# A similarity whose left side is not normalised, and a load moved behind the norms' row in SyncE's queue

## The reference, cut to what matters

```python
# x: after the attention block, plus its residual; _gn is a group norm
xf  = _gn(x).reshape(B, C, N).transpose(0, 2, 1)
xn  = xf / max(norm(xf, axis=-1), 1e-12)
sim = einsum('bnc,bmc->bnm', xn, xn)          # 1024 x 1024 per sample
val, idx = top_k(sim, 9)
v   = val / (val.sum(-1) + 1e-6)
# twice: xt = feat @ w; out[n] = sum_k v[n,k] * xt[idx[n,k]] + b
#        group norm with 4 groups, then silu
x   = x + out
```

## Time and profile before

| | before |
|---|---|
| median of 3 runs | 685.54 us (684.87 to 685.59) |
| the profiled execution | 687.54 us |
| its span, first to last instruction | 685.7 us |
| TensorE busy | 621.9 us (91%) |
| VectorE busy | 536.6 us (78%) |
| GpSimd busy | 499.2 us (73%) |
| ScalarE busy | 449.2 us (66%) |
| mean granted TensorE clock | 0.98 |

### The profile page before, as it was taken

One profiled execution on the slowest core, in us unless ns is written; L12 is line 12 of the kernel. 1 busy time (PEld: TensorE's weight loads), 2 busy tenths in 40 slices (PEclk: granted clock), 3 DMA queues, 4 the chain that ended last, 5 costly groups with the idle time before them and its releaser, 6 DMA issues.

```text
span 685.7 us, 12336 instructions
## 1 busy us (share of the span) xinstructions
PE 621.9 (91%) x3824; PEld 310.4 (45%) x3824; DVE 536.6 (78%) x1008; ACT 449.2 (66%) x942; POOL 499.2 (73%) x534
## 2 busy tenths in 40 slices
PE   8878899898999999898999999999999999899874
PEld 6654535353444535353544435353535444333441
DVE  3357879788898889797888988898898988857821
ACT  2356477685868767784868768786868686743321
POOL 0224877788797978879797978788897979786810
PEclk9999999999999999999999999999999999979997
DMA  3002533434353535444363634445353534353411
GB/s 94 1 17 46 115 72 79 88 83 96 81 110 69 109 77 110 80 90 92 80 109 62 113 79 108 87 87 100 91 94 63 109 77 98 74 108 78 63 32 31
DMA packets 148722, 55.76 MB, mean 81 GB/s; under 512 B 138008, under 2 KB 138512, under 8 KB 148656
## 3 DMA queue, kind: packets, MB, share of 16 engines
q1 hardware_dynamic: 148656, 54.97, 39.6%
HBM read 12.87 MB, written 4.32 MB: 25 GB/s over the span
## 4 chain that ended last, share of the span: by engine, by line
PE 33%; POOL 24%; issue 16%; DVE 10%; DMA 9%; ACT 7%; SPq 1%; POOLq 0%; ACTq 0%; DVEq 0%
PE pC L974 18%; POOL adj L389 10%; PE pS L930 5%; POOL adj L384 5%; DMA rbc<-rn_row 4%; DMA rn_row<-rnT 4%; ACT adj L527 2%; PE pB L775 2%; DVE kstat L607 2%; ACT ek L458 2%; POOL res L407 2%; PE pA L814 2%; POOL qn L348 2%; POOL xn L372 2%; DVE top L683 2%
## 5 line engine op out<-in xcount | busy, mean ns | idle before, releaser
L974 PE MATMUL pC<-adj,xt 128*64 128x512 f32 x992 | 233.1, 603 | 2.9 <-POOL adj L395 1.6
L389 POOL TENSOR_TENSOR adj<-maskT,adj 128x128 f32<-128x128 f16 (+3 forms) x127 | 163.5, 1287 | 27.0 <-DMA maskT<-mask 25.2
L683 DVE MAX8 top<-pS 128x8 f32<-128x1024 f32 x128 | 155.6, 1224 | 33.1 <-ACT adj L527 32.9
L701 DVE MATCH_REPLACE8 mask<-top,pS 128x1024 uint16<-128x1024 f32 x128 | 155.2, 1213 | 0.0
L930 PE MATMUL pS<-xn 64*128 64x512 f32 x256 | 146.9, 661 | 7.3 <-issue 6.5
L930 PE MATMUL pS<-xn,xsw 64*128 64x512 f32 x256 | 146.2, 662 | 2.9 <-DVE mask L701 2.9
L527 ACT COPY adj<-pS 128x1024 f32<-128x1024 f32 x128 | 128.3, 1003 | 30.3 <-PE pS L932 30.2
L384 POOL TENSOR_TENSOR adj<-maskT,adj 128x128 f32<-128x128 f16 (+6 forms) x111 | 128.4, 1157 | 0.0
L974 PEld LDWEIGHTS pC<-adj,xt 128*64 128x64 f32 x992 | 64.0, 137 | 103.3 <-issue 94.7
L395 POOL TENSOR_TENSOR adj<-adj,selves 128x128 f32<-128x128 f32 x127 | 58.5, 461 | 8.7
L932 PEld LDWEIGHTS pS<-mark,place 64*128 64x128 f16 x256 | 24.7, 97 | 77.3 <-issue 77.3
(11 more groups left out here) (154 smaller groups left out, 1097.0 us busy)
## 6 DMA issues: line engine op xcount, KB each, us to landing
xs<-x SPq DMA_DIRECT2D x32, 128.0 KB, 2.8
vbc<-v_row SPq DMA_DIRECT2D x32, 128.0 KB, 2.9
rbc<-rn_row SPq DMA_DIRECT2D x30, 128.0 KB, 2.9
xsw<-xn SPq DMA_DIRECT2D x30, 128.0 KB, 2.3
out<-res SPq DMA_DIRECT2D x30, 128.0 KB, 2.3
maskT<-mask SPq DMA_TRANSPOSE x128, 3.1
cst<-packed SPq DMA_DIRECT2D x1, 471.5 KB, 3.6
y1sw<-y SPq DMA_DIRECT2D x2, 128.0 KB, 2.3
```

The lines of the kernel that those rows point to most:

```text
L389: pool.tensor_tensor(above, m[:, r, 0:r + 1, :].bitcast(F16), above, ALU.mult).then_inc(done["upper"], 1)
L683: dve.max(top[b % 2][:, r, 0:TOP], pS[r % 2][:, :]).then_inc(done["tile_top"], 1)
L701: dve.match_replace(out=mask[n % MASKS][:, :], in_to_replace=top[b % 2][:, r, 0:TOP], in_values=pS[r % 2][:, :], imm_value=ONE_BITS).then_ ...
L974: mm = pe.matmul(ps[h * C:(h + 1) * C, 0:H], xt[:, t % NJ, t // NJ, :], adj[b % 2][:, t, h * H:(h + 1) * H], start=(t == 0), stop=(t == NT ...
```

## The change

Three things change.

The left side of the similarity is y1 in place of `xn` (and `xsw` is y1 with swapped halves). A block of `pS` then holds the similarity times the norm of the row's token. A positive factor per row leaves the order in the row alone, so the tops and masks are found as before; ScalarE's copy to `adj` takes the inverse norm as its scale, and VectorE multiplies the eight tops of each token by it once per sample. The constants are set anew so that the mark stays large beside the products. y1 and `rn` get two buffers each, y1sw goes, and `rn` waits for what still reads its older buffer.

The swapped copy now waits for y1 and no longer for `xn`. In SyncE's queue it is the first step of `unit`, at 111.8545, where it was the last, at 139.8554.

The load of a later sample moves in SyncE's queue from 0 to 19 behind the sample's begin: before it stood in front of the norms' row of the sample three earlier (122.814), now it stands behind it.

```diff
--- before.py
+++ after.py
@@ -15,9 +15,9 @@
 P = 128
 HEADS = 4
 TOP = 8
-XSCALE = 0.25
+XSCALE = 2.0 ** -12
 SSCALE = XSCALE * XSCALE
-MARK = -2.5 * SSCALE
+MARK = -2.5 / 16
 EPS = 1e-5
 ONE_BITS = 15360.0
 
@@ -34,8 +34,8 @@
           485.0099, 525.4191, 565.7534, 605.859]
 TIMES = {
     "sync": {
-        "attend": [0],
-        "unit": [122.814, 124.0739, 139.8554],
+        "attend": [19],
+        "unit": [111.8545, 122.814, 124.0739],
         "neighbours": [144.5435, 146.5376, 153.5254, 159.4181, 159.4182, 168.0831, 180.5052, 181.0079],
         "convolve": [199.2326, 199.2327, 265.073],
     },
@@ -155,13 +155,12 @@
 
         attn = sb("attn", [P, H])
         x1 = [sb(f"x1_{i}", [P, H]) for i in range(XBUFS)]
-        y1 = sb("y1", [P, H])
+        y1 = [sb(f"y1_{i}", [P, H]) for i in range(2)]
         sq = sb("sq", [P, H])
         xn = [sb(f"xn{i}", [P, H]) for i in range(2)]
-        y1sw = sb("y1sw", [P, H])
         xsw = [sb(f"xsw{i}", [P, H]) for i in range(2)]
         ssq = sb("ssq", [P, NT])
-        rn = sb("rn", [P, NT])
+        rn = [sb(f"rn{i}", [P, NT]) for i in range(2)]
         rnT = sb("rnT", [NT, P])
         rbc = sb("rbc", [P, H])
         st = {n: sb(f"st_{n}", [P, 16]) for n in ("in", "at", "mi", "g1", "g2")}
@@ -205,9 +204,9 @@
             ky_ps ky_copied m_ps m_copied att_ps att_copied
             at_stat at_aggr at_spread at_mean_ps at_minus at_dev at_veps at_rstd at_scale at_bias at_normed x1_ready
             mi_stat mi_aggr mi_spread mi_mean_ps mi_minus mi_dev mi_veps mi_rstd mi_bias y1_ready
-            sq_ready ss_ps ss_read rn_ready rows exchanged first_swapped rn_T rnT_copied rn_saved rn_back xn_ready swapped0 swapped1
+            sq_ready ss_ps ss_read rn_ready rows rn_T rnT_copied rn_saved rn_back xn_ready swapped0 swapped1
             xt1_ps xt1_copied sim_ps sim_copied self_ready tile_top tile_mask turned0 turned1 turned2 diagonal upper lower late_lower late_upper late_diagonal late_y late_res
-            v_tot v_rec v_T vT_copied v_saved v_back
+            top_scaled v_tot v_rec v_T vT_copied v_saved v_back
             g1_ps g1_read g1_stat g1_aggr g1_shift g1_spread g1_mean_ps g1_minus g1_dev g1_veps g1_rstd g1_scale g1_bias
             y2_ready xt2_ps xt2_copied tile_used
             g2_read g2_stat g2_aggr g2_shift g2_spread g2_mean_ps g2_minus g2_dev g2_veps g2_rstd g2_scale g2_bias
@@ -231,10 +230,6 @@
         def row_read(b):
 
             return of("xn_ready", 0) if b == 0 else of("rnT_copied", b - 1)
-
-        def swapped(b):
-
-            return (done["first_swapped"], 1) if b == 0 else of_buffer("swapped", b - 2 if b % 2 == 0 else b, 2, 32)
 
         def weave(engine, *stages):
             live = []
@@ -266,11 +261,12 @@
                                        .unsqueeze(0).broadcast_to([C, H]))
 
             def unit(b):
+                yield
+                sp.wait_ge(*of("y1_ready", b))
+                sp.wait_ge(*of("sim_ps", b - 2, NT))
+                for h in range(2):
+                    sp.dma_start(xsw[b % 2][(1 - h) * C:(2 - h) * C, :], y1[b % 2][h * C:(h + 1) * C, :]).then_inc(done[f"swapped{b % 2}"], 16)
                 if b == 0:
-                    yield
-                    sp.wait_ge(*of("y1_ready", b))
-                    for h in range(2):
-                        sp.dma_start(y1sw[(1 - h) * C:(2 - h) * C, :], y1[h * C:(h + 1) * C, :]).then_inc(done["exchanged"], 16)
                     return
                 yield
                 sp.wait_ge(*of("rnT_copied", b - 1))
@@ -280,11 +276,6 @@
                 sp.wait_ge(*of("xn_ready", b - 1))
                 for dma in spread(rn_row, rbc, b):
                     dma.then_inc(done["rn_back"], 16)
-                yield
-                sp.wait_ge(*of("xn_ready", b))
-                sp.wait_ge(*of("sim_ps", b - 2, NT))
-                for h in range(2):
-                    sp.dma_start(xsw[b % 2][(1 - h) * C:(2 - h) * C, :], xn[b % 2][h * C:(h + 1) * C, :]).then_inc(done[f"swapped{b % 2}"], 16)
 
             def neighbours(b):
                 for r in range(NT):
@@ -359,7 +350,9 @@
                 rstd(b, "mi")
                 yield
                 pool.wait_ge(*of("ss_read", b, 2))
-                pool.tensor_tensor(rn[:, :], ssq[:, :], minus_half[:, :], ALU.pow).then_inc(done["rn_ready"], 1)
+                pool.wait_ge(*of("sim_copied", b - 2, NT))
+                pool.wait_ge(*of("v_tot", b - 2))
+                pool.tensor_tensor(rn[b % 2][:, :], ssq[:, :], minus_half[:, :], ALU.pow).then_inc(done["rn_ready"], 1)
                 yield
                 if b == 0:
                     return
@@ -367,9 +360,7 @@
                 pool.wait_ge(*of("rn_back", b - 1, 32))
                 pool.wait_ge(*of("xt1_ps", b - 2))
                 pool.wait_ge(*of("sim_ps", b - 2, NT))
-                if b > 2:
-                    pool.wait_ge(*swapped(b - 2))
-                pool.tensor_tensor(xn[b % 2][:, :], y1[:, :], rbc[:, :], ALU.mult).then_inc(done["xn_ready"], 1)
+                pool.tensor_tensor(xn[b % 2][:, :], y1[b % 2][:, :], rbc[:, :], ALU.mult).then_inc(done["xn_ready"], 1)
 
             def weights(b):
                 a, m = adj[b % 2], maskT[b % 2]
@@ -499,12 +490,12 @@
                 deviation(b, "mi", pB)
                 yield
                 act.wait_ge(*of("mi_bias", b))
-                act.wait_ge(*of("xn_ready", b - 1))
-                act.activation(y1[:, :], x1[b % XBUFS][:, :], ACT.Identity, bias=st["mi"][:, 15:16],
+                act.wait_ge(*of("sim_ps", b - 2, NT))
+                act.activation(y1[b % 2][:, :], x1[b % XBUFS][:, :], ACT.Identity, bias=st["mi"][:, 15:16],
                                scale=st["mi"][:, 13:14]).then_inc(done["y1_ready"], 1)
                 yield
                 act.wait_ge(*of("y1_ready", b))
-                act.activation(sq[:, :], y1[:, :], ACT.Square).then_inc(done["sq_ready"], 1)
+                act.activation(sq[:, :], y1[b % 2][:, :], ACT.Square).then_inc(done["sq_ready"], 1)
 
             def itself(b):
                 for r in range(NT):
@@ -522,9 +513,10 @@
                     n = NT * b + r
                     yield
                     act.wait_ge(*of_tile("sim_ps", n))
+                    act.wait_ge(*of("rn_ready", b))
                     if b >= 2:
                         act.wait_ge(*of_tile("tile_used", n - 2 * NT))
-                    act.copy(adj[b % 2][:, r, :], pS[r % 2][:, :]).then_inc(done["sim_copied"], 1)
+                    act.activation(adj[b % 2][:, r, :], pS[r % 2][:, :], ACT.Copy, scale=rn[b % 2][:, r:r + 1]).then_inc(done["sim_copied"], 1)
 
             def silu(b, tag, src, dst, signal):
                 yield
@@ -665,10 +657,7 @@
                 yield
                 if b == 0:
                     dve.wait_ge(done["rows"], 1)
-                    dve.tensor_tensor(xn[0][:, :], pB[:, :], y1[:, :], ALU.mult).then_inc(done["xn_ready"], 1)
-                    dve.wait_ge(done["rows"], 2)
-                    dve.wait_ge(done["exchanged"], 32)
-                    dve.tensor_tensor(xsw[0][:, :], pC[:, :], y1sw[:, :], ALU.mult).then_inc(done["first_swapped"], 1)
+                    dve.tensor_tensor(xn[0][:, :], pB[:, :], y1[0][:, :], ALU.mult).then_inc(done["xn_ready"], 1)
                 else:
                     dve.wait_ge(*of("rn_T", b - 1))
                     dve.wait_ge(*of("rn_saved", b - 2, 16))
@@ -683,6 +672,12 @@
                     dve.max(top[b % 2][:, r, 0:TOP], pS[r % 2][:, :]).then_inc(done["tile_top"], 1)
                 yield
                 dve.wait_ge(*of("tile_top", b, NT))
+
+                dve.wait_ge(*of("tile_mask", b, NT))
+                dve.wait_ge(*of("rn_ready", b))
+                best = top[b % 2][:, :, 0:TOP]
+                dve.tensor_tensor(best, best, rn[b % 2][:, :].unsqueeze(2).broadcast_to([P, NT, TOP]), ALU.mult).then_inc(done["top_scaled"], 1)
+                dve.wait_ge(*of("top_scaled", b))
                 dve.wait_ge(*of("ss_read", b, 2))
                 dve.tensor_reduce(vtot[:, :], top[b % 2][:, :, :], AX.X, ALU.add).then_inc(done["v_tot"], 1)
                 dve.wait_ge(*of("v_tot", b))
@@ -906,27 +901,26 @@
                     pe.wait_ge(*of("g1_veps", b - 2))
                 if b == 0:
 
-                    for bank, other in ((pB, 0), (pC, 1)):
-                        for j in range(NJ):
-                            for h in range(2):
-                                t = (h ^ other) * NJ + j
-                                mm = pe.matmul(bank[h * C:(h + 1) * C, j * P:(j + 1) * P], rn[:, t:t + 1].broadcast_to([P, C]), ident,
-                                               start=True, stop=True)
-                        mm.then_inc(done["rows"], 1)
-                else:
-                    pe.transpose(pB[0:NT, P:2 * P], rn[:, :], ident).then_inc(done["rn_T"], 1)
+                    for j in range(NJ):
+                        for h in range(2):
```

(11 more changed lines are left out.)

## The result

The changed kernel takes 831.75 us (median of 4 runs, 830.08 to 835.19) where the kernel before, run beside it, takes 685.57. The ratio is 1.2124, with a 95% interval of 1.2063 to 1.2186. The profiled execution has a span of 828.3 us, against 685.7. The forecast was 820, in a range of 795 to 850.

A forecast was written before the change was run, and what follows sets the result against it. The prediction took a closed loop through several engines and DMA, one sample per 37.55 us, as the bound. 123 + 17 + 1.4 + 3.3 - 9 - 2 = 134 us on 687.54 gave 821.5, median 820, range 795 to 850.

The forecast's parts named there:

- The swapped copy holds SyncE's queue: SyncE waits some 9 us for y1 before mask 2, v row and vbc: 8.8 us per period, 123 us in all.
- the v row until SyncE goes on: Term of the stall's sum on SyncE: 1.95 us from the v row's issue to vbc's issue.
- from vbc's issue to g1: Term of the stall's sum: 3.54 us from vbc's issue to its reader on VectorE, taken from the norms' row.
- The upper bound for it, 3.47: Slowest v row allowed for on SyncE, from one behind two loads and a mask: 21 us more in all.
- Rival B: The swap does not hold SyncE's queue, y1 being ready after mask 1; the kernel gets faster, 680 us; chance 0.03.
- TensorE's clock: An 8.8 us hole before ek's transposes lowers TensorE's clock each period: 1.2 us per period, 17 us in all.
- the scaled copy: ScalarE's similarity copy with a per-partition scale: 0.1 us for one copy on the loop per period, 1.4 us in all.
- The norms' row: Without the load in front, the row on SyncE takes 1.20 us, not 2.06: 11 samples x 0.86, 9 us less.
- The product of the tops: One VectorE product over 128x64 per sample after mask 7, in idle time: nothing; without that cover 14 x 0.3 = 4.
- the earlier first similarity: TensorE's first similarity no longer waits for a swap of xn: 2 us less in all.
- Sample 1: Its swap holds mask 2 of sample 0 on SyncE, so GpSimd's norms start later: 3.3 us more.

The follow-up runs named there:

- e5: The changed kernel with the swapped copy of y1 issued behind mask 5, where the kernel before had it: 685.31 us, ratio 0.9955.
- e7: The changed kernel with 40 unread matmuls of zeros behind the sums of squares of samples 2 to 15: 838.54 us, ratio 1.2171.
- e2: The changed kernel with the swapped copy of y1 issued behind the spreading of the norms' row: 698.13 us, ratio 1.0182.
- e9: The changed kernel with 15 unread fp32 matmuls of 256 columns behind the sums of squares of samples 2 to 15: 815.82 us, ratio 1.19.
- e1: The kernel before with only its load moved from 0 to 19 behind the sample's begin: 676.18 us, ratio 0.985.
- e8: The changed kernel with the load back at 0, in front of the norms' row: 832.83 us, ratio 1.2069.
- e6: e5 without VectorE's product of the tops with the norms: 682.05 us, ratio 0.9886.
- e10: The changed kernel without VectorE's product of the tops with the norms: 831.98 us, ratio 1.2135.

## Why the prediction was right, point by point

**The swapped copy holds SyncE's queue: right, in mechanism and size.** 8.8 us per period were summed, 8.85 measured (-0.04 to 8.81). Inside the sum two terms were off and cancel: the v row until SyncE goes on took 1.55, not 1.95 (402.01 to 403.56), and from vbc's issue to g1 it took 3.90, not 3.54 (403.56 to 407.46). My worry that two copies of 128 KB just ahead would slow the row was not borne out: it takes 1.6 in e5 as well, where they are not ahead of it. Why it took 1.95 in the kernel before stays open. The upper bound for it, 3.47, rested on a misreading. I had put that row down to two loads and a mask in front, but eleven other rows with the same in front take 1.7 to 2.3; what it has besides is a 16 KB instruction packet, as the slow v rows of e7 have. e2 and e5 move that step alone and take the loss away. Rival B needed y1 some 9 us earlier; it came no earlier.

**TensorE's clock: right.** 1.2 us per period for the clock and 0.1 for the scaled copy were summed; k's maximum to rnT grew by 1.36, and e9 gives 1.12 of it back. The copy itself (now L519) takes 1.105 on the mean, 0.10 more than before, which is the difference of the earlier trace rows. The rule of the Trainium skill that I set beside it (TensorE: Matmul & The Clock Gate, section Terms: throttled time times one minus the ratio) gives more. The clock was low from about 404.7 to 414.9 (0.58, 0.50 and 0.64 in the three windows, 10.2 us at half), so an estimate by that rule is 5.1 us a period. This trace doesn't agree: TensorE stood idle for 5.9 of these 10.2 us, until 410.58, and what the low clock cost the loop was 1.1.

**The norms' row: right size, wrong cause in this kernel.** rnT to xn fell by 0.71, as summed (0.7 to 0.9). e1 shows that the load's place is worth this in the kernel before, 9 us. But e8 shows that in the changed kernel it is worth nothing, because the stall had already moved the row away from the load. The two parts of the change are not additive, and I had added them. The constant of about 2.0 us that I had cited from the Trainium skill (DMA: Bandwidth & Descriptors, section Anatomy of one DMA) is given there for transfers that GpSimd issues. The rows here are issued by SyncE, so that their 1.20 us disagrees with it, as I wrote, was too much said.

**The product of the tops: the term that failed.** The forecast put it at nothing, under 0.7 us long and in VectorE's idle time. It takes 1.24 on the mean, up to 1.82, and xn to x1 grew by 0.70 where I had expected it to fall by 0.15, the earlier first similarity. One period of the changed kernel shows how, a stretch of VectorE's queue and GpSimd's step that waits for it:

```profile
378.26 1.55 DVE L679 TENSOR_TENSOR top<-top,rn 128x64 f32<-128x64 f32 x1
...
381.02 2.35 DVE L672 MAX8 top<-pS 128x8 f32<-128x1024 f32 x2
...
388.60 0.54 POOL L331 TENSOR_TENSOR st_g<-st_g,minus_half 128x1 f32<-128x1 f32 x1 [0.76 <-DVE st_g L574]
```

The idle time that I had counted on, 0.88 ahead of the tops, was there and is used up: the tops now follow without a gap. The product is longer than that cover, VectorE runs on late, and GpSimd waits 0.76 for it, where the same step of the kernel before did not wait (at 362.08). e6 takes 0.67 of the 0.70 away in the one kernel, e10 in seven periods of twelve in the other. So the place was read rightly and the length was not; why it is so long is told at the end.

**Sample 1: too small.** 3.3 us were summed and y1 of sample 2 came 5.6 later. GpSimd began mask 2 at 74.29, not 73.0, and did three products and a diagonal ahead of the norms where I counted two products: they start at 77.68, not 75.6.

```profile
74.29 0.92 POOL L380 TENSOR_TENSOR adj<-maskT,adj 128x384 f32<-128x384 f16 x1 [6.50 <-DMA maskT<-mask]
75.28 0.45 POOL L386 TENSOR_TENSOR adj<-adj,selves 128x128 f32<-128x128 f32 x1
75.69 0.91 POOL L375 TENSOR_TENSOR adj<-maskT,adj 128x384 f32<-128x384 f16 x1
76.57 1.16 POOL L380 TENSOR_TENSOR adj<-maskT,adj 128x512 f32<-128x512 f16 x1
77.68 1.65 POOL L355 TENSOR_TENSOR rn<-ssq,minus_half 128x8 f32<-128x8 f32 x1
```

**The end** got only 6.5 us longer behind y1 of sample 15, where I had counted a whole period's 9.3. Between the profiled spans the sum lacks 9 us: 2.3 at the start, 9 in the 13 periods and -3 at the end. The 9 are 13 x 0.85 = 11 from xn to x1, less the 1.6 that came back between x1 and y1. So the start and the end, both mis-sized, nearly cancel, and that the total came so close owes something to luck. The measured median lies 12 above the forecast of 820, about 3 of them because the profiled execution of the changed kernel was below its median by 1.7 and not above it by 2.0.

## What to carry to other kernels

A wait in an in-order queue costs what stands behind it, not what it issues. Before moving a step forward, look in the trace for the real time of what it waits for and for the real time of its new neighbours; due times of a planner only give the order. Walk the loop of one period once: if the step that becomes late is a link of it, the stall counts in full, once per sample, and it can take TensorE's clock with it if the hole falls on TensorE, as it did here for 1.1 us of each 10.1. And a gain and a loss on the same loop need not add up: the stall had removed the contention that the other half of the change was made against.

## What the runs showed of the hardware

**VectorE's small product of two SBUF operands ends when GpSimd's running operation ends.** In the changed kernel:

```profile
473.51 1.82 DVE L679 TENSOR_TENSOR top<-top,rn 128x64 f32<-128x64 f32 x1
...
755.18 0.23 DVE L679 TENSOR_TENSOR top<-top,rn 128x64 f32<-128x64 f32 x1
```

```profile
473.34 1.91 POOL L339 TENSOR_TENSOR qn<-qe,qrec 128x1024 f32<-128x1024 f32 x1
...
753.45 1.65 POOL L380 TENSOR_TENSOR adj<-maskT,adj 128x768 f32<-128x768 f16 x1
755.18 0.54 POOL L386 TENSOR_TENSOR adj<-adj,selves 128x128 f32<-128x128 f32 x1
```

The first starts inside GpSimd's qn, which ends at 475.25, and ends itself at 475.33. The second starts when GpSimd is just between two operations and takes 0.23. Of the 16 products of this trace 15 end 0.08 us behind the GpSimd operation that was running when they started, and so do e5's 16. VectorE's reduction from PSUM (L599) shows no such thing, 1.21 to 1.23 each time. The Trainium skill, SBUF — State Buffer, section SBUF: two separate sides, states it: the port pair shared by VectorE and GpSimd is an exclusive lock for a whole instruction, taken by a VectorE operation with two SBUF inputs against a GpSimd operation that reads SBUF. This trace agrees, 0.23 free and up to 1.82 behind qn.

**The time that a row of 4 KB takes to SyncE's next step depends on what else runs.** The norms' row takes 1.2 or 2.1 us, by whether SyncE was done issuing 256 KB 1.8 or 0.3 us ahead of it (e8). The v row, right behind a mask's transposing copy, mostly takes 1.6 in the changed kernel and its variants and 1.95 to 2.0 in the kernel before and in e1. Every row of either kind above 2.6 us, in all traces, had one 16 KB instruction packet in its time, and no row without one took that long.
